# The diagonal key blocks of a head pair in one maximum job

## The reference

```python
scores = einsum('bhqd,bhkd->bhqk', qh, kh) / sqrt(hd)        # hd = 32
qi = arange(Sq)[:, None] + (Sk - Sq)                         # Sk - Sq = 1089
causal = arange(Sk)[None, :] <= qi
scores = where(causal, scores, -10000.0)
attn = softmax(scores, axis=-1)
out = einsum('bhqk,bhkd->bhqd', attn, vh)
x = x + tanh(g_xattn) * out
...
t = silu(g) * u                                              # g, u, y: quantised linear layers
x = x + tanh(g_ffn) * y
```

## Time and profile before

| | |
|---|---|
| time, median of 3 runs (lowest, highest) | 1294.32 us (1292.91, 1298.19) |
| the profiled execution: its span | 1287.7 us |
| mean granted clock of TensorE | 0.914 of full speed |
| busy: TensorE matmul, VectorE, ScalarE, GpSimd | 1057.5, 851.6, 647.7, 328.6 us |
| matmuls | 5642, of them 832 at L720 and 320 at L724 |
| reductions at L988 | 416, 427.2 us |

### The profile page before, as it was taken

How to read it: one execution, slowest core, us unless ns; L and a number is a source line. 1 busy time by engine, 2 the same in 40 slices (tenths; PEclk the granted TensorE clock), 3 DMA queues, 4 the chain that set the end, 5 groups by cost and what they waited for, 6 DMA issues and landing times.

```text
span 1287.7 us, 16709 instructions
## 1 busy us (share of the span) xinstructions
PE 1057.5 (82%) x5642; PEld 368.6 (29%) x5642; DVE 851.6 (66%) x1406; ACT 647.7 (50%) x1326; POOL 328.6 (26%) x334
## 2 busy tenths in 40 slices
PE   4687897788889898998989888989898999894443
PEld 1222232222223232323333322323332323232221
DVE  8677766567757666666676676667776576434874
ACT  2345546455555546464646455554645464662321
POOL 3012313233102213031222131222223031432452
PEclk9998878877999899999999999989999999996767
DMA  6913322122472221212731211114621110000000
GB/s 145 182 54 94 99 56 59 51 53 56 84 96 51 59 60 26 60 27 54 112 65 41 69 26 42 43 26 92 96 59 27 34 26 9 1 9 9 8 9 16
DMA packets 155100, 70.40 MB, mean 55 GB/s; under 512 B 111032, under 2 KB 142856, under 8 KB 155016
## 3 DMA queue, kind: packets, MB, share of 16 engines
q1 hardware_dynamic: 153256, 63.57, 23.3%
q0 software_dynamic: 1760, 5.77, 1.5%
HBM read 39.08 MB, written 4.19 MB: 34 GB/s over the span
## 4 chain that ended last, share of the span: by engine, by line
PE 60%; DVE 15%; issue 12%; ACT 7%; POOL 5%; DMA 1%; SPq 0%; POOLq 0%; ACTq 0%; DVEq 0%
PE ps L797 23%; PE ps L774 11%; DVE mch L988 7%; PE ps L720 6%; PE ps L817 6%; ACT pr L585 3%; PE ps L836 3%; DVE kTl L979 2%; ACT kTh L545 2%; PE ps L724 2%; PE ps L746 1%; DVE ff L914 1%; PE ps L748 1%; POOL t_q L405 1%; PE ps L827 1%
## 5 line engine op out<-in xcount | busy, mean ns | idle before, releaser
L585 ACT ACTIVATE pr<-ps 128x512 f32<-128x512 f32 (+4 forms) x832 | 397.2, 530 | 280.1 <-PE ps L774 153.6
L988 DVE TENSOR_REDUCE mch<-ps 128x2 f32<-128x1024 f32 (+4 forms) x416 | 427.2, 1057 | 142.0 <-PE ps L720 123.9
L797 PE MATMUL ps<-pr,vf 128*33 128x512 f32 (+4 forms) x1664 | 416.1, 581 | 0.0
L774 PE MATMUL ps<-qst,kst 97*128 97x512 f16 (+4 forms) x832 | 256.4, 375 | 33.3 <-ACT pr L585 25.8
L720 PE MATMUL ps<-kTh,qTh 32*128 32x512 f16 (+4 forms) x832 | 153.7, 382 | 86.5 <-DVE kTl L979 47.1
L774 PEld LDWEIGHTS ps<-qst,kst 97*128 97x128 f16 (+1 forms) x832 | 70.7, 101 | 304.1 <-ACT pr L585 184.1
L417 POOL TENSOR_TENSOR xs<-xs,upd 128x256 f32<-128x256 f32 x32 | 23.3, 727 | 328.4 <-DVE upd L1031 328.4
L720 PEld LDWEIGHTS ps<-kTh,qTh 32*128 32x128 f16 x832 | 37.9, 92 | 220.9 <-issue 74.5
L797 PEld LDWEIGHTS ps<-pr,vf 128*33 128x33 f32 (+1 forms) x1664 | 62.9, 112 | 86.3 <-issue 60.6
L817 PE MATMUL ps<-wgu,t_T 128*128 128x352 bf16 x448 | 80.8, 327 | 2.7 <-ACT t_T L606 1.5
L1066 DVE SCALAR_TENSOR_TENSOR ff<-ps,scs,wsb 128x352 f32<-128x352 f32 x56 | 32.7, 584 | 72.9 <-PE ps L817 72.6
(11 more groups left out here) (146 smaller groups left out, 1164.5 us busy)
## 6 DMA issues: line engine op xcount, KB each, us to landing
kst<-kTh SPq DMA_DIRECT2D x128, 100.1 KB, 2.2
ksrc<-in_ctx SPq DMA_DIRECT2D x16, 768.0 KB
vf<-in_ctx SPq DMA_DIRECT2D x48, 256.0 KB, 4.0
kst<-kTl SPq DMA_DIRECT2D x64, 100.1 KB, 2.2
xs<-in_x SPq DMA_DIRECT2D x16, 256.0 KB, 4.1
qst<-qTh SPq DMA_DIRECT2D x128, 32.0 KB, 1.9
out<-xs SPq DMA_DIRECT2D x16, 256.0 KB, 3.2
ff<-in_L_ffn_w_down SPq DMA_DIRECT2D x4, 704.0 KB, 4.2
```

The lines of the kernel that those rows point to most:

```text
L585: nc.scalar.activation(pr[0:kn, n % NP, q0:S], ps[0:kn, j, q0:S], ACT.Exp, scale=SCALE).then_inc(ex_done, 1)
L774: last = nc.tensor.matmul(ps[0:kn, j, q0:S], kst[s][0:ST, r, k0:k0 + kn], qst[s][0:ST, r, q0:S], start=True, stop=(t < DT))
L797: nc.tensor.matmul(ps[64 * j:64 * j + VW, 2 + pp % 2, q0:S], vf[0:kn, t, h, :], pr[0:kn, n % NP, q0:S], start=(t == 0), stop=(t == NT - 1) ...
L988: nc.vector.tensor_reduce(mch[:, qt, 2 * hp:2 * hp + 2, c], both[:, :, 0:k1 - k0], AX.X, ALU.max).then_inc(dve_free, 1)
```

## The change

The list of jobs changes. The four query tiles' jobs stop at the diagonal block, so that they have no masked columns. A 13th job per head pair takes the four diagonal blocks: for each query tile and head one product of 128 queries with the 128 keys of its block, four side by side in a head's bank, eight products in all. Then one mask product per head adds the triangle to all four blocks: the identity is read four times over as a moving operand of 512 columns. One reduction gives 4 x 2 maxima, which go to chunk 3 of `mch`. A head pair had 13 jobs (3, 3, 3 and 4 for the four query tiles) and has 13 (3, 3, 3, 3 and the diagonal one).

```diff
         for qt in range(QT):
-            end = NEAR + P * (qt + 1)
+            end = NEAR + P * qt
             for c in range((end + 511) // 512):
                 chunks.append((hp, qt, c, 512 * c, min(512 * c + 512, end)))
+        chunks.append((hp, None, 3, NEAR, SK))
...
-            d0 = NEAR + P * qt
-            lo, hi = max(k0, d0), min(k1, d0 + P)
             for i in range(2):
                 rows = slice(HD * (2 * hp + i), HD * (2 * hp + i + 1))
-                last = nc.tensor.matmul(slot(job)[:, 512 * i:512 * i + k1 - k0], qTh[rows, gg % 2, qt * P:(qt + 1) * P],
-                                        kTh[rows, gg % 2, k0:k1], start=True, stop=(hi <= lo))
-            if hi > lo:
+                if qt is not None:
+                    last = nc.tensor.matmul(slot(job)[:, 512 * i:512 * i + k1 - k0], qTh[rows, gg % 2, qt * P:(qt + 1) * P],
+                                            kTh[rows, gg % 2, k0:k1], start=True, stop=True)
+            if qt is None:
+                for q in range(QT):
+                    for i in range(2):
+                        rows = slice(HD * (2 * hp + i), HD * (2 * hp + i + 1))
+                        nc.tensor.matmul(slot(job)[:, 512 * i + P * q:512 * i + P * (q + 1)], qTh[rows, gg % 2, q * P:(q + 1) * P],
+                                         kTh[rows, gg % 2, k0 + P * q:k0 + P * (q + 1)], start=(q == 0), stop=False)
                 for i in range(2):
-                    last = nc.tensor.matmul(slot(job)[:, 512 * i + lo - k0:512 * i + hi - k0], maskT[:, :],
-                                            idb[:, lo - d0:hi - d0], start=False, stop=True)
+                    last = nc.tensor.matmul(slot(job)[:, 512 * i:512 * i + S], maskT[:, :], idb[:, :].unsqueeze(1).broadcast_to([P, QT, P]),
+                                            start=False, stop=True)
             last.then_inc(mx_mm, 1)
...
             both = slot(("max", gg, j)).rearrange("p (a b) -> p a b", a=2)
-            nc.vector.tensor_reduce(mch[:, qt, 2 * hp:2 * hp + 2, c], both[:, :, 0:k1 - k0], AX.X, ALU.max).then_inc(dve_free, 1)
+            if qt is None:
+                nc.vector.tensor_reduce(mch[:, :, 2 * hp:2 * hp + 2, c].rearrange("p t h -> p h t"),
+                                        both.rearrange("p h (t n) -> p h t n", t=QT), AX.X, ALU.max).then_inc(dve_free, 1)
+            else:
+                nc.vector.tensor_reduce(mch[:, qt, 2 * hp:2 * hp + 2, c], both[:, :, 0:k1 - k0], AX.X, ALU.max).then_inc(dve_free, 1)
```

## The result

The changed kernel took 1313.03 us (median of 4 runs, 1308.76 to 1318.19) against 1296.26 us for the kernel before (4 runs). The ratio is 1.0154, with a 95% interval of 1.0117 to 1.0191. In twelve more runs it took 1309.27 us (1303.74 to 1318.19), ratio 1.0126 (1.0088 to 1.0165). It is slower by 1.3 to 1.5%; the prediction had 1288.3 and a range up to 1302. Ratios leave out runs that lie more than 1.5% above the fastest of their kernel; the kernel before has such runs, 17 of the 60 timed beside the experiments, at 1307 to 1331 us and mean clocks of 0.866 to 0.896, so that it is at times as slow as the changed kernel by itself.

A forecast was written before the change was run, and what follows sets the result against it. TensorE, busy 82% of the span and 60% of the chain, was taken to bound the kernel. -0.43 us a group gave -6.5 us over 15 groups, 0.5 taken back: 1294.3 - 6 = 1288.3 us, range 1277 to 1302.

The forecast's parts named there:

- the rival of VectorE's lateness: Late diagonal reduction makes TensorE wait 1.1 us at 30 places, 33 us if none is covered, 1321 us; chance 0.12.
- The wait at step 9: TensorE's wait for L979, the staged keys' low half, before the diagonal job: near 1.45 us instead of 1.16.
- The rival of exposed weight loads: Diagonal scores' weight loads don't hide under 128-column products: 0.74 us instead of 0.40, +10 us, 1298.5 us; chance 0.18.
- the estimate of 0.64: Diagonal scores at 0.64 us instead of 0.40 by the skill page's weight-load rule, 7 us more in all.
- -0.66 - 0.19: Second half of a group: us saved by removed masks and narrower scores in the third, sixth and ninth jobs.
- 0.15 taken back at step 19: Charge of 0.15 us a group because TensorE arrives earlier and waits longer before the pair's end in the second half.
- -0.43: Forecast change per group in us, from -0.23 in the second half and -0.20 in the first; -6.5 us over 15 groups.
- VectorE late becomes TensorE's wait: Rival: the later diagonal reduction holds up TensorE, 1.1 us at 30 places, 33 us if uncovered, 1321 us; chance 0.12.
- A few of them either way are in my range: Slow-clock stretches of TensorE, some 1.6 us of lost clock each, a few more or fewer counted within the forecast's range.
- a sign that the forecast fails: The forecast fails if the mean granted clock moves by more than 0.01 or the diagonal job takes over 1.3 us.
- The rival with the clock: The clock falls at step 9 as at step 6: eight more slow stretches at 1.6 us, 1301 us; chance 0.10.
- The 6.6 us between span and median: The runs' median stands 6.6 us above the profiled span; added unchanged to the forecast span of 1281.7 us.

The follow-up runs named there:

- experiments 2 and 8: Overwritten filler products ahead of TensorE's waits. 2: kernel before 1271.27 us, changed kernel 1271.72. 8: kernel before 1257.11, diagonal job third 1244.41, ahead of waits 1249.16.
- (6): Kernel before without masks in each pair's third, sixth and ninth jobs: ratio 0.9969; kernel before with two overwritten 512-column products ahead of the thirteenth job's scores: 1.0105.
- (4): Changed kernel with overwritten columns, as many as the old masks had, ahead of the third, sixth, ninth and twelfth jobs: 1309.19 us, ratio 1.0112.
- (5): Changed kernel with two overwritten 384-column products ahead of each of two jobs where TensorE waits for nothing: 1328.13 us, ratio 1.0230.

## Why the prediction was wrong

- **The prices were right or too high.** A removed mask with its 128 narrower columns was to give 0.22 + 0.063, and gives 0.27. The diagonal job was to cost 1.07 and costs 0.87; the scores take 0.34 where the bounds were 0.26 and 0.52, and the two heads' products do run side by side. The reduction was costed at 1221 ns and is 1222. The matmuls' waits for the maximum reductions are 42.2 us in all against 37.9, those ahead of weight loads 138.5 against 128.1: the rival of VectorE's lateness, 33 us, did not come. The wait at step 9 was to be near 1.45 and is 1.35. The rival of exposed weight loads (0.74 for the scores) is out, and so is the estimate of 0.64 made from the rule of the Trainium skill's page "TensorE: Matmul & The Clock Gate", section "LDWEIGHTS (loading the stationary operand)": 0.34 for eight loads and products does not agree with it.
- **The first step that failed is what lies on the path.** "-0.66 - 0.19" was let through whole in the second half, with 0.15 taken back at step 19; in fact VectorE's slots took back 0.27 at steps 5, 14 and 16, 0.8 a group. The diagonal job cost 0.56 and 0.46 instead of 0.76 and 0.62. The sum is +0.2 instead of -0.43. The rival "VectorE late becomes TensorE's wait" described another cause (the diagonal job's late reduction): behind steps 9 and 19 the table shows no new wait. The waits came where TensorE was early, not where VectorE was late. This step is 0.64 us a group, nearly 10 us of the 24.7 by which the forecast missed.
- **The second, and the larger, is the clock.** "A few of them either way are in my range" made it noise around the forecast. Between the two profiles it was 54 us more at the low level, 22 to 25 us of the 23.5; between the medians it is some 14 of the 16.8. The mean clock moved by 0.019, which the prediction had named as a sign that the forecast fails. The rival with the clock had the price of a low stretch about right (1.6 us; with one of them a group of before takes 67.3 us instead of 66.0, with three 70.6) but counted on eight new ones at step 9 alone, with a chance of 0.10. In the last ten groups that prepare a next one, two began at step 9 where the kernel before has none; at step 6 they began in 8 groups instead of 5, at steps 14 and 15 in 8 instead of 6, and at step 2 in 6 instead of 7, most of them longer. The rows on which the prediction said that the clock holds at step 9 end at 455 us, ahead of the end of that wait (455.77); the trace of before bears it out none the less, with no low stretch until 470 us.
- **The 6.6 us between span and median were not overhead.** The run of the profiled execution after took 1313.03 us with a span of 1311.2, 1.8 more. The profiled execution of before was one of the better runs (clock 0.914); its low time, on which the sum was built, was that of a good run.

**What stays open.** Shown is that low clock costs the time (experiments 2 and 8), and that the changed kernel has more of it than the kernel before: the main loop has 0.90 to 0.92 in the five profiles with the diagonal job at the end of the pair and no filler, and 0.92 to 0.94 in the four with the old list of jobs. Why the change brings more of it is not shown. Either part of it alone moves the time by about its work at equal clock (6). Work put back at the light jobs does not bring the clock back (4), and another length of the group, the one tried, left it where it was (5). The pattern in the kernel before is telling: its groups 6, 7, 8 and 10, 11, 12 (from 0) take 67.3, 70.6, 66.0 and again 67.3, 70.6, 66.0 us, while in the changed kernel two groups in a row are 71.6 and 71.7 us, both at 0.90:

```profile
857.80:929.40 71.60, 64.37 (x337) 21.25 (x338) 45.87 (x73) 37.62 (x77) 16.33 (x17) 0.90 0.38 71
929.40:1001.10 71.70, 64.43 (x338) 21.39 (x338) 49.03 (x83) 37.62 (x77) 17.34 (x18) 0.90 0.27 52
```

That suggests that where a wait falls in time matters beside its length, and that the kernel before sat in a lucky rhythm which nearly any edit breaks. This is argued, not shown.

## What to carry to other kernels

Where TensorE sets the time and its granted clock moves, compare repeating stretches at equal clock first; only there does a sum of instruction prices hold, and the clock's share is a separate term, here several times larger than the other. Put a long job ahead of a wait, not behind it: the same operations made the kernel 1.3% slower in one place and 2.1% faster in another, and a group at full clock 66.23 and 65.30 us. Before counting a saving, look one or two jobs on for the wait at which the engine will now arrive early.

## What the runs showed of the hardware

- Useless matmuls in TensorE's waits made a kernel faster: 18 products of 384 columns a group, 1.5%; with six more at steps 0 and 1, 3.1%. They hold the granted clock, 0.95 and 0.98 in the main loop against 0.94 in the best and 0.90 in the worst of the others.
- Leaving out 320 mask products, some 26 us of the chain, left the time where it was (ratio 1.0019); the main loop's clock was 0.92 instead of 0.94.
- Eight products of 32 rows and 128 columns for two row groups, each with its own weight load, took 0.34 us, 43 ns each, so the two heads' products and their loads overlap; a mask product with the identity read four times over as moving operand ran like any other of 512 columns, 410 ns.
- A reduction over 1,024 elements costs the same with 8 outputs, written with a stride, as with 2: 1222 and 1222 ns in the changed kernel.
